# Moving the second copy of the un-normed result's high half from ScalarE to GpSimd

## The chip, the cores and the metric

The kernel runs on one core of one Trainium2 chip. The metric is the device time of that core in microseconds (us); the time given is the median of three runs. One more execution was profiled, and all rows below come from it. Batches, pairs, steps, blocks and rope operations are counted from 0; the steps' pairs are numbered through all batches, 0 to 31.

## The reference, cut to what matters

One transformer layer on x of shape (4, 1024, 256): a layer norm, multi-head latent attention with 16 heads, and beside it a linear layer with binarised weights. Both are added to x.

```
xn = layernorm(x)
kv_c = xn @ W_kvd + b_kvd                    # 64 wide
q_c  = xn @ W_qd + b_qd                      # 192 wide
keys_c, values = heads(kv_c @ W_ku + b_ku), heads(kv_c @ W_vu + b_vu)   # 16 heads x 128
keys_r = rope(heads(kv_c @ W_kr + b_kr))     # 16 heads x 64
queries_c, queries_r = heads(q_c @ W_qu + b_qu), rope(heads(q_c @ W_qr + b_qr))
scores = (concat(queries) @ concat(keys).T) / sqrt(192), causal
ctx = softmax(scores) @ values
x + ctx @ W_o + b_o + (xn @ binarised(W_ffn).T + b_ffn)
```

All is computed in float32 precision: a number is split into a high half (fp32r) and a low half (the number less its high half), and products are added up as high x high, high x low and low x high.

## The kernel before, in words

Weights are folded in a prologue (to about 130 us), so that attention works in the 64-wide space of kv_c. Then comes the main part: 4 batches x 8 pairs of heads = 32 steps m; each step has 4 blocks n, so there are 128 blocks g = 4m + n. A block takes two tiles of 128 queries, w = 0 (the long one) and w = 1 (the short one), for both heads of the pair. Every engine has its own `sequence(g)`, an order of calls written out by hand for n = 0, 1, 2 and 3. The calls name earlier blocks too: in block g TensorE works on the scores of g, turns and weighs the probabilities of g - 1 and g - 2, and makes the output of g - 2 and g - 3.

What one (block, w) passes through at its end:

- TensorE's `weigh_group` (L1369, L1370) adds up probabilities times kv_c in the PSUM tile `u_ps`: the un-normed result u, two heads side by side.
- ScalarE's `u_high` (L707) writes its high half to `u_hi[w]`, 128 partitions x 256.
- DVE's `u_low` (L941) writes the low half of the upper 64 partitions to partitions 0 to 63 of `u_pair[w]`.
- ScalarE's `u_again` (L716) copies partitions 0 to 63 of `u_hi[w]` to partitions 64 to 127 of `u_pair[w]`, the second copy of the high half. It counts up `u_copied`.
- TensorE's `output` waits for `u_ready` (from DVE) and `u_copied`, multiplies with the folded values' weights (L1389, L1390) into `o_ps`, and DVE's `accumulate` (L971) adds that to the result.

GpSimd (POOL) works in the main part on the rotary positions of the next pair: `step(m)` prepares pair m + 1. Its chain is ten `rope` operations, numbered 0 to 9 (L301), and two `low_keys` (L311), in the order rope 0, 1, 2, low_keys 1, rope 3, 4, 5, 6, 7, 8, low_keys 0, rope 9. rope 0 waits for the first swap of halves (`swapped<-k_rope`, four DMAs from SyncE's queue), rope 3 for the second (`swapped<-q_x`, `q_y`), which SyncE starts when ScalarE has evacuated the query projection q_y (L621). low_keys 1 waits for `k_hi` (L671) and rope 8 and 9 for `q_hi` (L675), all from ScalarE; ScalarE's `high_queries` in turn wait for rope 6 and 7. The next pair's scores on TensorE wait for rope 8, low_keys 0 and rope 9. In pair 5 of each batch but the last, `residual` (L456, eight additions) follows behind rope 9; in pairs 3 and 4 a few small operations and in pair 6 `down_low` stand in the chain too.

Every semaphore wait on an engine holds back all that is written behind it there.

Of the kernel before, what the change touches and what calls it, by code (L numbers as in the profile page):

```python
# [26 lines left out]
F32 = mybir.dt.float32  # L27
F32R = mybir.dt.float32r
BF16 = mybir.dt.bfloat16
ACT = mybir.ActivationFunctionType  # L30
# [4 lines left out]
P = 128  # L35
NB, SEQ, HID = 4, 1024, 256
# [32 lines left out]
STEPS = NB * PAIRS  # L69
# [25 lines left out]
def is_block(g):  # L95
    return 0 <= g < STEPS * BLOCKS
# [22 lines left out]
def build(nc, x, W_kvd, b_kvd, W_ku, b_ku, W_vu, b_vu, W_kr, b_kr, W_qd, b_qd, W_qu, b_qu, W_qr, b_qr,  # L119
# [6 lines left out]
    with ExitStack() as ctx:  # L126
# [320 lines left out]
        def _(pool):  # L447
# [43 lines left out]
            def down_low(b, k):  # L491
# [3 lines left out]
                pool.wait_ge(down_lo, b * 2 + k + 1)  # L495

            def step(m):

                b, pair = divmod(m, PAIRS)
                more = b + 1 < NB  # L500
                if m + 1 == STEPS:
                    return
                rope(pool, m + 1, range(0, 3))
                low_keys(pool, m + 1, 1)
                if more and pair in (3, 4):
                    pool.wait_ge(k_lo_ready, (m + 1) * 2 + 1)
                    (combine, refine)[pair - 3](b + 1)
                rope(pool, m + 1, range(3, 8))
                if more and pair == 6:
                    pool.wait_ge(rope_step, (m + 1) * ROPE_OPS + 8)  # L510
                    down_low(b + 1, 0)
                    down_low(b + 1, 1)
                rope(pool, m + 1, range(8, 9))
                low_keys(pool, m + 1, 0)
                rope(pool, m + 1, range(9, 10))
                if more and pair == 5:
                    pool.wait_ge(rope_step, (m + 1) * ROPE_OPS + ROPE_OPS)
                    residual(b + 1)
                    pool.wait_ge(residual_ready, (b + 2) * NT)
# [77 lines left out]
        def _(act):  # L597
# [106 lines left out]
            def u_high(g, w):  # L704
                if is_block(g):
                    act.wait_ge(u_full, g * 2 + w + 1)
                    act.activation(u_hi[w][:, :], u_ps[:, 0:2 * P], ACT.Identity).then_inc(u_hi_ready, 1)  # L707
                if w == 1 and (g + 1) % (PAIRS * BLOCKS) == 0 and g + 1 < STEPS * BLOCKS:
                    natural_high((g + 1) // (PAIRS * BLOCKS))

            def u_again(g, w):

                if not is_block(g):
                    return
                act.wait_ge(u_hi_ready, g * 2 + w + 1)
                act.activation(u_pair[w][64:P, :], u_hi[w][0:64, :].bitcast(F32), ACT.Identity).then_inc(u_copied, 1)  # L716

            def sequence(g):

                b, pair, n = g // (PAIRS * BLOCKS), g // BLOCKS % PAIRS, g % BLOCKS  # L720
                if n == 0:
                    evacuate(g, ROPE_K)
                    turned_high(g - 1, 0)
                    u_again(g - 2, 0)
                    u_high(g - 2, 1)
# [9 lines left out]
                    u_high(g - 1, 0)  # L735
                    u_again(g - 2, 1)
                    exponent(g, 2)
                    turned_high(g - 1, 4)
                    u_again(g - 1, 0)
                    if pair == 6:  # L740
# [11 lines left out]
                elif n == 1:  # L752
                    exponent(g, 0)
                    u_again(g - 2, 1)
                    if pair == 6:
# [8 lines left out]
                    if pair == 5:  # L764
                        next_apply(b + 1, 3)
                    u_again(g - 1, 0)
                    if pair == 4:
# [5 lines left out]
                elif n == 2:  # L773
                    exponent(g, 0)
                    turned_high(g - 1, 3)
                    if pair == 6:
                        next_down_high(b + 1, 1)
                    u_again(g - 2, 1)
                    exponent(g, 1)
# [8 lines left out]
                    turned_high(g, 0)  # L788
                    u_again(g - 1, 0)
                    high_queries(g, 0)  # L790
                    u_high(g - 1, 1)
                    turned_high(g, 1)
                else:
# [7 lines left out]
                    if pair == 5:  # L801
                        next_left("transpose", b + 1, 1)
                    u_again(g - 2, 1)
                    turned_high(g - 1, 4)
# [807 lines left out]
```

## Time and profile before

| what | value |
|---|---|
| median of 3 runs | 1487.29 us (1485.34 to 1489.63) |
| the profiled execution | 1487.06 us, of which its span is 1485.3 us |
| TensorE matmul busy | 1416.0 us, 95% |
| DVE busy | 1155.7 us, 78% |
| ScalarE (ACT) busy | 1204.2 us, 81% |
| GpSimd (POOL) busy | 981.4 us, 66% |

The span is what the rows cover, from the first instruction to the last; 1.8 us of the time lie outside it. In a row of a timeline the first number is the start and the second the duration, in us; in square brackets stands how long the engine was idle before it, and who released it. PE is the matmul and PEld the weight load of TensorE.

### The profile page before, as it was taken

To read this page: it belongs to the slowest core of one execution; us is meant where nothing else is said; L and a number is where in the kernel's file an instruction comes from. 1 tells how busy PE (TensorE), PEld (TensorE's weight loads), DVE (VectorE), ACT (ScalarE), POOL (GpSimd) and SP (SyncE) were. 2 spreads that over 40 slices of the span, in tenths; PEclk is the share of its full clock that TensorE was granted. 3 is DMA by queue.
4 is the path that set the end of the run, shared out by engine and by line. 5 is a ranking of instruction groups with operands and counts; after the bars stand their busy time and mean duration, and the time that the engine had idled before them with its cause. 6 is when DMAs were issued, how large, how long until landed. Compare 5 with 4: busy or idle time off the path is not lost.

```text
span 1485.3 us, 27605 instructions
## 1 busy us (share of the span) xinstructions
PE 1416.0 (95%) x9849; PEld 1281.7 (86%) x9849; DVE 1155.7 (78%) x2755; ACT 1204.2 (81%) x2553; POOL 981.4 (66%) x553
## 2 busy tenths in 40 slices
PE   3688999999999999999999999999999999999997
PEld 3467899999799989999889998999889999989987
DVE  2465888888677889888677888888677888878888
ACT  2345888899788888899778898889868888888886
POOL 5254777777656777777766777776767677677750
PEclk9778999999999999999999999999999999999999
DMA  8545121222142232211233221222132422211110
GB/s 232 172 138 153 49 76 43 60 61 61 54 111 64 69 89 62 61 54 55 61 72 100 78 86 51 61 61 61 46 74 67 111 61 62 62 46 42 49 30 29
DMA packets 41550, 110.48 MB, mean 74 GB/s; under 512 B 7574, under 2 KB 18119, under 8 KB 41415
## 3 DMA queue, kind: packets, MB, share of 16 engines
q1 hardware_dynamic: 37126, 95.09, 24.1%
q0 software_dynamic: 3232, 12.58, 2.4%
q8 instruction: 80, 1.31, 0.4%
q10 hardware_dynamic: 1056, 1.05, 0.3%
q14 instruction: 56, 0.45, 0.1%
HBM read 48.92 MB, written 13.63 MB: 42 GB/s over the span
## 4 chain that ended last, share of the span: by engine, by line
PE 76%; ACT 8%; POOL 5%; DVE 4%; DMA 3%; issue 2%; SPq 1%; POOLq 0%; DVEq 0%; ACTq 0%
PE turn L1351 14%; PE ring L1296 10%; PE u_ps L1369 7%; PE ring L1328 7%; PE ring L1326 7%; PE ring L1327 7%; PE u_ps L1370 7%; PE o_ps L1389 3%; PE o_ps L1390 3%; ACT probs L693 3%; PE ring L1258 2%; PE ring L1250 2%; PE ring L1309 2%; ACT probs_hi L702 1%; POOL k_rope L301 1%
## 5 line engine op out<-in xcount | busy, mean ns | idle before, releaser
L925 DVE TENSOR_SCALAR_CACHE_REDUCE probs<-ring,c_t 128x1024 f32<-128x1024 f32 (+7 forms) x512 | 413.8, 809 | 105.1 <-PE ring L1328 100.9
L935 DVE TENSOR_TENSOR probs_lo<-turn,probs_hi 128x512 fp32r<-128x512 f32 (+1 forms) x640 | 401.5, 631 | 70.0 <-ACT probs_hi L702 64.8
L702 ACT ACTIVATE probs_hi<-turn 128x512 fp32r<-128x512 f32 (+1 forms) x640 | 350.5, 550 | 113.2 <-PE turn L1351 107.4
L693 ACT ACTIVATE probs<-probs,row_min 128x1024 f32<-128x1024 f32 (+7 forms) x512 | 394.3, 771 | 12.1 <-DVE probs L925 9.6
L1351 PE MATMUL turn<-ident,probs 128*128 128x128 f32 x2304 | 386.2, 275 | 9.6 <-ACT probs L693 7.3
L1351 PEld LDWEIGHTS turn<-ident,probs 128*128 128x128 f32 x2304 | 285.9, 140 | 37.5 <-ACT probs L693 13.4
L1369 PE MATMUL u_ps<-probs_hi,kv_nat 128*128 128x256 f32 x1152 | 314.6, 302 | 0.3 <-DVE probs_lo L935 0.3
L1370 PE MATMUL u_ps<-probs_lo,kv_nat 128*128 128x256 f32 x1152 | 289.3, 281 | 0.0
L1326 PE MATMUL ring<-k_hi,q_hi 128*128 128x512 f32 (+2 forms) x768 | 280.2, 365 | 0.0
L1328 PE MATMUL ring<-k_hi,q_lo 128*128 128x512 f32 (+2 forms) x768 | 264.0, 344 | 0.0
L1327 PE MATMUL ring<-k_lo,q_hi 128*128 128x512 f32 (+2 forms) x768 | 263.4, 343 | 0.0
L971 DVE SCALAR_TENSOR_TENSOR acc<-o_ps,row_inv,acc 128x256 f32<-128x256 f32 x480 | 230.4, 480 | 34.6 <-PE o_ps L1390 30.2
L1369 PEld LDWEIGHTS u_ps<-probs_hi,kv_nat 128*128 128x128 f32 x1152 | 219.3, 190 | 1.7 <-DVE probs_lo L935 0.5
L1370 PEld LDWEIGHTS u_ps<-probs_lo,kv_nat 128*128 128x128 f32 x1152 | 218.6, 190 | 0.0
L311 POOL TENSOR_TENSOR k_lo<-k_rope,k_hi 64x1024 fp32r<-64x1024 f32 x62 | 148.2, 2391 | 51.5 <-ACT k_hi L671 49.1
L301 POOL TENSOR_TENSOR k_rope<-k_rope,cos 128x1024 f32<-128x1024 f32 x31 | 74.4, 2401 | 156.5 <-DMA swapped<-k_rope 156.3
L301 POOL TENSOR_TENSOR q_x<-q_x,cos 64x1024 f32<-64x1024 f32 x31 | 74.2, 2395 | 136.1 <-DMA swapped<-q_x 136.1
L1328 PEld LDWEIGHTS ring<-k_hi,q_lo 128*128 128x128 f32 x768 | 145.1, 189 | 13.9
L1326 PEld LDWEIGHTS ring<-k_hi,q_hi 128*128 128x128 f32 x768 | 146.9, 191 | 7.4
L301 POOL TENSOR_TENSOR swapped<-swapped,sin 128x1024 f32<-128x1024 f32 x62 | 148.8, 2401 | 4.9
L1327 PEld LDWEIGHTS ring<-k_lo,q_hi 128*128 128x128 f32 x768 | 145.8, 190 | 7.2
L1389 PE MATMUL o_ps<-wv,u_hi 128*128 128x256 f32 x512 | 143.4, 302 | 4.3 <-DVE acc L971 2.3
(210 smaller groups left out, 2607.8 us busy)
## 6 DMA issues: line engine op xcount, KB each, us to landing
wp<-wp_scratch SPq DMA_DIRECT2D x31, 640.0 KB, 4.2
swapped<-k_rope SPq DMA_DIRECT2D x128, 128.0 KB, 2.3
wv<-wv_scratch SPq DMA_DIRECT2D x31, 512.0 KB, 3.4
swapped<-q_y SPq DMA_DIRECT2D x64, 128.0 KB, 2.3
swapped<-q_x SPq DMA_DIRECT2D x64, 128.0 KB, 2.4
wp_scratch<-wp_parts POOLq DMA_DIRECT2D x7, 640.0 KB, 3.5
x_sb<-in_L_attn_x SPq DMA_DIRECT2D x4, 1024.0 KB, 6.5
k_hi<-qb_kv_hi SPq DMA_DIRECT2D x16, 256.0 KB, 3.7
```

What stands on the lines that cost most here:

```text
L301: engine.tensor_tensor(to, a, b, op).then_inc(rope_step, 1)
L693: act.activation(p, p, ACT.Exp, scale=-1.0, bias=row_min[:, r:r + 1], accum_out=row_sum[:, g % 4, w, h:h + 1]).then_inc(exp_ready, 1)
L702: act.activation(probs_hi[:, r % 4, 0:width], turn[r % 2][:, 0:width], ACT.Identity).then_inc(turned_hi, 1)
L925: dve.tensor_scalar(probs_of(g, w, h), ring[slot_of(entry)][:, KEY_COLUMN[qt]:KEY_COLUMN[qt] + keys], c_t[b % 2][:, qt, ds(pair * 2 + h, 1 ...
L935: dve.tensor_tensor(probs_lo[:, r % 4, 0:width], turn[r % 2][:, 0:width], probs_hi[:, r % 4, 0:width].bitcast(F32), ALU.subtract).then_inc ...
L971: dve.scalar_tensor_tensor(out=acc[:, qt, :], in0=o_ps[:, h, :], scalar=inv, in1=start[:, qt, :], op0=ALU.mult, op1=ALU.add).then_inc((acc ...
L1326: pe.matmul(to, qh, kh[:, keys], start=not masked, stop=False, skip_group_check=masked)
L1327: pe.matmul(to, qh, kl[:, keys], start=False, stop=False, skip_group_check=masked)
L1328: mm = pe.matmul(to, ql, kh[:, keys], start=False, stop=True, skip_group_check=masked)
L1351: mm = pe.transpose(turn[r % 2][:, (2 * t + h) * P:(2 * t + h + 1) * P], probs_of(g, w, h)[:, kt * P:(kt + 1) * P], ident[:, :])
L1369: pe.matmul(u_ps[:, 0:2 * P], kv_nat[:, kt, :], probs_hi[:, r % 4, cols], start=(kt == 0), stop=False)
L1370: mm = pe.matmul(u_ps[:, 0:2 * P], kv_nat[:, kt, :], probs_lo[:, r % 4, cols], start=False, stop=(kt == qt))
```

## The change: what it does

`u_again` leaves ScalarE's sequence in all its places and becomes a function of GpSimd's program, a `tensor_copy`. GpSimd makes eight such copies in a step: (g - 2, 0) and (g - 2, 1) before rope 0, (g - 1, 0) behind rope 0, (g - 1, 1) behind low_keys 1, (g, 0) behind rope 3, (g, 1) behind rope 4, (g + 1, 0) behind rope 6 and (g + 1, 1) behind rope 7, where g is the first block of the step. A copy waits for the rope operation before it, for `u_hi_ready`, for the output of the block before (`o_full`), and then for its own end (`u_copied`). ScalarE's `u_high` gets a wait for the copy of the block before, since its tile is now read on another engine.

```diff
@@ -494,18 +494,47 @@
                                    ALU.subtract).then_inc(down_lo, 1)
                 pool.wait_ge(down_lo, b * 2 + k + 1)
 
+            def u_again(g, w, roped=None):
+
+                if not is_block(g):
+                    return
+                if roped is not None:
+                    pool.wait_ge(rope_step, roped)
+                pool.wait_ge(u_hi_ready, g * 2 + w + 1)
+                if g >= 1:
+
+                    pool.wait_ge(o_full, g * 2 + w - 1)
+                pool.tensor_copy(u_pair[w][64:P, :], u_hi[w][0:64, :].bitcast(F32)).then_inc(u_copied, 1)
+                pool.wait_ge(u_copied, g * 2 + w + 1)
+
             def step(m):
 
                 b, pair = divmod(m, PAIRS)
-                more = b + 1 < NB
+                more, g, roped = b + 1 < NB, m * BLOCKS, (m + 1) * ROPE_OPS
+                u_again(g - 2, 0, m * ROPE_OPS + ROPE_OPS)
+                u_again(g - 2, 1)
                 if m + 1 == STEPS:
+                    for later in range(g - 1, STEPS * BLOCKS):
+                        for w in range(2):
+                            u_again(later, w)
                     return
-                rope(pool, m + 1, range(0, 3))
+                rope(pool, m + 1, range(0, 1))
+                u_again(g - 1, 0, roped + 1)
+                rope(pool, m + 1, range(1, 3))
                 low_keys(pool, m + 1, 1)
+                pool.wait_ge(k_lo_ready, (m + 1) * 2 + 1)
+                u_again(g - 1, 1)
                 if more and pair in (3, 4):
                     pool.wait_ge(k_lo_ready, (m + 1) * 2 + 1)
                     (combine, refine)[pair - 3](b + 1)
-                rope(pool, m + 1, range(3, 8))
+                rope(pool, m + 1, range(3, 4))
+                u_again(g, 0, roped + 4)
+                rope(pool, m + 1, range(4, 5))
+                u_again(g, 1, roped + 5)
+                rope(pool, m + 1, range(5, 7))
+                u_again(g + 1, 0, roped + 7)
+                rope(pool, m + 1, range(7, 8))
+                u_again(g + 1, 1, roped + 8)
                 if more and pair == 6:
                     pool.wait_ge(rope_step, (m + 1) * ROPE_OPS + 8)
                     down_low(b + 1, 0)
@@ -704,16 +733,12 @@
             def u_high(g, w):
                 if is_block(g):
                     act.wait_ge(u_full, g * 2 + w + 1)
+                    if g >= 1:
+
+                        act.wait_ge(u_copied, g * 2 + w - 1)
                     act.activation(u_hi[w][:, :], u_ps[:, 0:2 * P], ACT.Identity).then_inc(u_hi_ready, 1)
                 if w == 1 and (g + 1) % (PAIRS * BLOCKS) == 0 and g + 1 < STEPS * BLOCKS:
                     natural_high((g + 1) // (PAIRS * BLOCKS))
-
-            def u_again(g, w):
-
-                if not is_block(g):
-                    return
-                act.wait_ge(u_hi_ready, g * 2 + w + 1)
-                act.activation(u_pair[w][64:P, :], u_hi[w][0:64, :].bitcast(F32), ACT.Identity).then_inc(u_copied, 1)
 
             def sequence(g):
 
@@ -721,7 +746,6 @@
                 if n == 0:
                     evacuate(g, ROPE_K)
                     turned_high(g - 1, 0)
-                    u_again(g - 2, 0)
                     u_high(g - 2, 1)
                     turned_high(g - 1, 1)
                     if pair == 4:
...
```

The seven other calls of `u_again` in ScalarE's `sequence` are removed likewise.

The first place is GpSimd's program from rope 5 of pair 6 of the first batch (`swapped,sin`), past the residual, to the first operations for pair 7. Before:

```order
L301 TENSOR_TENSOR swapped<-swapped,sin 128x1024
L301 TENSOR_TENSOR q_x<-q_x,swapped 64x1024
L301 TENSOR_TENSOR q_y<-q_y,swapped 64x1024
L301 TENSOR_TENSOR q_lo<-q_x,q_hi 128x1024
L311 TENSOR_TENSOR k_lo<-k_rope,k_hi 64x1024
L301 TENSOR_TENSOR q_lo<-q_y,q_hi 128x1024
L456 TENSOR_TENSOR x_sb<-x_sb,bias_out 128x256 x8
L301 TENSOR_TENSOR k_rope<-k_rope,cos 128x1024
L301 TENSOR_TENSOR swapped<-swapped,sin 128x1024
```

The same place now, where L507 is the copy:

```order
L301 TENSOR_TENSOR swapped<-swapped,sin 128x1024
L301 TENSOR_TENSOR q_x<-q_x,swapped 64x1024
L507 CAST u_pair<-u_hi 64x256
L301 TENSOR_TENSOR q_y<-q_y,swapped 64x1024
L507 CAST u_pair<-u_hi 64x256
L301 TENSOR_TENSOR q_lo<-q_x,q_hi 128x1024
L311 TENSOR_TENSOR k_lo<-k_rope,k_hi 64x1024
L301 TENSOR_TENSOR q_lo<-q_y,q_hi 128x1024
L456 TENSOR_TENSOR x_sb<-x_sb,bias_out 128x256 x8
L507 CAST u_pair<-u_hi 64x256 x2
L301 TENSOR_TENSOR k_rope<-k_rope,cos 128x1024
L507 CAST u_pair<-u_hi 64x256
```

Two copies stand inside the chain here (two more stand ahead of the piece, behind `q_x,cos` and `q_y,cos`), and the two that end the step's blocks stand behind the residual.

The second place is ScalarE's program around the start of that same pair (the row `k_rope<-ring,bias_p` is the first call of a step). Before:

```order
L716 ACTIVATE u_pair<-u_hi 64x256
L702 ACTIVATE probs_hi<-turn 128x256
L693 ACTIVATE probs,row_sum<-probs,row_min 128x640
L707 ACTIVATE u_hi<-u_ps 128x256
L693 ACTIVATE probs,row_sum<-probs,row_min 128x512
L621 ACTIVATE k_rope<-ring,bias_p 128x1024
L702 ACTIVATE probs_hi<-turn 128x512
L716 ACTIVATE u_pair<-u_hi 64x256
L707 ACTIVATE u_hi<-u_ps 128x256
```

Now:

```order
L731 ACTIVATE probs_hi<-turn 128x256
L722 ACTIVATE probs,row_sum<-probs,row_min 128x640
L739 ACTIVATE u_hi<-u_ps 128x256
L722 ACTIVATE probs,row_sum<-probs,row_min 128x512
L650 ACTIVATE k_rope<-ring,bias_p 128x1024
L731 ACTIVATE probs_hi<-turn 128x512
L739 ACTIVATE u_hi<-u_ps 128x256
```

The copies are gone from ScalarE and nothing else changes its place there. The order on TensorE, DVE and SyncE is the same as before.

## Rows read from the trace of the kernel before

**Rows 1.** Stretch 170 to 1430: busy us (instructions) by engine, TensorE clock, DMA, GB/s.

```profile
170.00:1430.00 1260.00, 1247.62 (x8849) 1140.40 (x8848) 1021.69 (x2419) 1088.36 (x2286) 893.39 (x426) 1.00 0.25 66
```

**Rows 2.** Waits of the whole span: total us, times, longest us.

```profile
POOL q_x L301 <- DMA swapped<-q_x: 136.1, 31, 6.3
PE turn L1351 <- ACT probs L693: 7.3, 10, 1.1
```

**Rows 3.** Grouped lines of ScalarE: busy us, mean ns, idle before.

```profile
L716 ACT ACTIVATE u_pair<-u_hi 64x256 fp32r<-64x256 f32 x256 | 106.7, 417 | 6.2
```

**Rows 4.** Timeline, GpSimd, ScalarE, TensorE, around the start of pair 3.

```profile
217.20 1.12 ACT L621 ACTIVATE q_y<-ring,bias_p 128x1024 f32<-128x1024 f32 x1 [0.54 <-PE ring L1296]
222.64 2.39 POOL L301 TENSOR_TENSOR q_x<-q_x,cos 64x1024 f32<-64x1024 f32 x1 [4.51 <-DMA swapped<-q_x]
233.62 1.06 ACT L675 ACTIVATE q_hi<-q_x 128x1024 fp32r<-128x1024 f32 x1
240.01 2.39 POOL L301 TENSOR_TENSOR q_lo<-q_y,q_hi 128x1024 fp32r<-128x1024 f32 x1
240.43 0.37 ACT L707 ACTIVATE u_hi<-u_ps 128x256 fp32r<-128x256 f32 x1
243.02 0.42 ACT L716 ACTIVATE u_pair<-u_hi 64x256 fp32r<-64x256 f32 x1
244.23 0.37 PE L1389 MATMUL o_ps<-wv,u_hi 128*128 128x256 f32 x1
```

**Rows 5.** Grouped lines of GpSimd by form: busy us, mean ns.

```profile
L456 POOL TENSOR_TENSOR x_sb<-x_sb,bias_out 128x256 f32<-128x256 f32 x32 | 24.3, 799 | 0.2
L533 POOL CAST wp<-qr 128x128 fp32r<-128x128 f32 x2 | 0.6, 288 | 0.1
L534 POOL CAST wp<-kr 128x64 fp32r<-128x64 f32 x2 | 0.5, 230 | 0.0
```

**Rows 6.** Timeline, DVE and weight load, near the end.

```profile
1475.69 0.42 DVE L941 TENSOR_TENSOR u_pair<-u_ps,u_hi 64x256 fp32r<-64x256 f32 x1 [1.25 <-ACT u_hi L707]
1476.16 0.19 PEld L1389 LDWEIGHTS o_ps<-wv,u_hi 128*128 128x128 f32 x1 [1.13 <-DVE u_pair L941]
```

**Rows 7.** Timeline, last rope and output, at first and last of 17 boundaries.

```profile
200.63 2.39 POOL L301 TENSOR_TENSOR q_lo<-q_y,q_hi 128x1024 fp32r<-128x1024 f32 x1
204.43 0.36 PE L1389 MATMUL o_ps<-wv,u_hi 128*128 128x256 f32 x1
...
1392.30 2.40 POOL L301 TENSOR_TENSOR q_lo<-q_y,q_hi 128x1024 fp32r<-128x1024 f32 x1
1396.55 0.36 PE L1389 MATMUL o_ps<-wv,u_hi 128*128 128x256 f32 x1
```

**Rows 8.** Timeline, last rope and output at the start of pair 10.

```profile
544.68 2.41 POOL L301 TENSOR_TENSOR q_lo<-q_y,q_hi 128x1024 fp32r<-128x1024 f32 x1
547.59 0.37 PE L1389 MATMUL o_ps<-wv,u_hi 128*128 128x256 f32 x1
```

**Rows 9.** Timeline, GpSimd and TensorE around the first residual.

```profile
356.36 2.41 POOL L301 TENSOR_TENSOR q_lo<-q_x,q_hi 128x1024 fp32r<-128x1024 f32 x1 [0.81 <-ACT q_hi L675]
361.37 2.40 POOL L301 TENSOR_TENSOR q_lo<-q_y,q_hi 128x1024 fp32r<-128x1024 f32 x1
363.85 5.59 POOL L456 TENSOR_TENSOR x_sb<-x_sb,bias_out 128x256 f32<-128x256 f32 x8
366.71 0.36 PE L1389 MATMUL o_ps<-wv,u_hi 128*128 128x256 f32 x1
```

**Rows 10.** Timeline, last rope and output at the start of pair 8.

```profile
458.94 2.40 POOL L301 TENSOR_TENSOR q_lo<-q_y,q_hi 128x1024 fp32r<-128x1024 f32 x1
466.36 0.36 PE L1389 MATMUL o_ps<-wv,u_hi 128*128 128x256 f32 x1
```

**Rows 11.** Stretches around 1144, columns as in Rows 1.

```profile
1142.00:1144.00 2.00, 1.06 (x12) 0.83 (x9) 1.61 (x4) 0.97 (x3) 1.92 (x2) 1.00 0.03 8
1145.40:1148.80 3.40, 3.40 (x17) 3.40 (x17) 1.89 (x5) 2.10 (x5) 2.98 (x2) 0.51 0.00 0
```

More of the change, by code:

```diff
@@ L735, in sequence @@
                     u_high(g - 1, 0)
-                    u_again(g - 2, 1)
                     exponent(g, 2)
                     turned_high(g - 1, 4)
-                    u_again(g - 1, 0)
                     if pair == 6:
@@ L753, in sequence @@
                     exponent(g, 0)
-                    u_again(g - 2, 1)
                     if pair == 6:
@@ L765, in sequence @@
                         next_apply(b + 1, 3)
-                    u_again(g - 1, 0)
                     if pair == 4:
@@ L777, in sequence @@
                         next_down_high(b + 1, 1)
-                    u_again(g - 2, 1)
                     exponent(g, 1)
@@ L788, in sequence @@
                     turned_high(g, 0)
-                    u_again(g - 1, 0)
                     high_queries(g, 0)
@@ L802, in sequence @@
                         next_left("transpose", b + 1, 1)
-                    u_again(g - 2, 1)
                     turned_high(g - 1, 4)
```

## Prediction

> **What bounds the kernel now.** I read the busy time by stretch first. In the main part TensorE's matmuls are busy for 1247.6 of 1260 us at the full granted clock of 2.4 GHz, ScalarE for 1088.4 and GpSimd for 893.4 [rows 1]. TensorE sets the time; all its waits there come to 12.4 us. ScalarE has slack on average, and so has GpSimd. Taking work from ScalarE can give back no more than a share of those 12.4 us, while whatever makes TensorE wait comes on top in full. So the question is when the copies are finished now, and when TensorE asks for them.
>
> The list of waits comes next. GpSimd waits 136.1 us in 31 times for the second swap, 4.4 us each, and TensorE's longest item behind ScalarE is 7.3 us [rows 2]. GpSimd's idle time thus lies before rope 3. The timeline of an ordinary pair shows what follows [rows 4]: from rope 3 at 222.64 to rope 9 at 240.01 eight operations run with no gap, 17.37 us or seven times 2.48, so the chain is GpSimd's own from there on. It ends at 242.40, and TensorE starts the output of block g - 2, w = 0 at 244.23. ScalarE had finished u_hi for it at 240.80 and made the copy at 243.02 to 243.44, in time.
>
> **ScalarE's part.** It loses 256 operations of 417 ns, 106.7 us [rows 3]. None of that lies on the path by itself. What it can return are TensorE's waits, at most 12.4 us [rows 1]. Those behind ScalarE's probabilities are 7.3 us in all, the prologue's included [rows 2], and I take 4 us back.
>
> **The price of a copy on GpSimd.** No row shows this copy. The nearest are GpSimd's casts to fp32r: 288 ns for 128 elements, 230 ns for 64 [rows 5], a slope of 0.9 ns an element, which extends to 0.41 us for 256. The lower end is 0.29 us, the cast with half as many elements; the upper is the 256-element addition with its 0.80 us mean [rows 5]. A larger price because partitions 0 to 63 go to 64 to 127 isn't excluded either, and is held to be inside the upper end. I take 0.41, from the nearest rows in kind. With 0.07 us for the next instruction's start (2.48 less the 2.39 to 2.41 of an operation) a copy inside the chain moves all behind it by 0.48 us.
> The Trainium skill's page GPSIMD Engine Reference, section 4.1, Engine selection, speaks against elementwise work on GpSimd, about twice as slow with two inputs, but holds one input to be roughly line rate. [...] No run here shows it yet.
>
> **Where the copies fall.** Five matter. Four stand between rope 3 and rope 9, and move the end of rope 9 by 4 x 0.48 = 1.92 us. The one that TensorE asks for next, (g - 2, 0) of the next step, stands behind rope 9, though its u_hi has long been there. It ends 0.07 + 0.41 later; a weight load starts 0.05 us after what it waits for [rows 6], and I allow 0.04 more to its matmul. So the output can start 2.49 us after the end of rope 9 in the old timeline. The old timeline gives it less:
>
> - Ordinary boundaries between two pairs: 1.83 us at pair 3 [rows 4], 1.41 at the first of them and 1.85 at the last [rows 7]. There are 17 (pairs 2 to 5, 9, 11 to 13, 17, 18, 20, 21, 25 to 27, 29 and 30). TensorE comes to wait 0.66, 1.08 and 0.64 us at those three. Where rope 8 had waited for q_hi (5, 13, 21) the chain takes up part of the slip. I take 0.6 us as the mean: 17 x 0.6 = 10.2.
> - Five boundaries with less room (1, 10, 19, 28, 31), as the second swap came late: 547.59 - 547.09 = 0.50 us at pair 10 [rows 8]. TensorE waits 2.0 there: 5 x 2.0 = 10.0.
> - Three boundaries with the residual between rope 9 and the copy (6, 14, 22). Rope 9 ends at 363.77, the residual takes 5.59 + 0.08 on top, and the output stood at 366.71, which is 2.94 us behind rope 9 [rows 9]. The copy allows it at 5.67 + 2.49 = 8.16, less 0.74 of the 0.81 us that rope 8 had waited [rows 9]: a wait of 8.16 - 0.74 - 2.94 = 4.48. 3 x 4.5 = 13.5.
> - Six with room to spare (7, 8, 15, 16, 23, 24): 5.02 us at pair 8 [rows 10]. Nothing.
>
> The sum is 33.7 us. The chain of the next pair starts from a swap that follows TensorE's projections and ScalarE's evacuation, so each wait shifts TensorE and the next chain together; the next boundary is short by the same amount again, not by more or less.
>
> **The clock.** In the stretch 1142 to 1144 TensorE is busy 1.06 of 2 us, and 1145.4 to 1148.8 runs at a granted 0.51, its 1.2 GHz level [rows 11]. Half speed over 3.4 us costs 1.7 us. The three waits of 4.5 us are longer than that idle stretch, so I add 3 x 1.7 = 5.
>
> **What I count at nothing.** Rope 2 ends one copy (0.48 us) later, and k_hi with it; ScalarE's 0.54 us wait for the projection of q_y covers this [rows 4]. With no cover it would be 0.5 us in 31 pairs, 15 us. The second swap on SyncE's queue waits for rope 2 too, but the evacuation of q_y ends at 218.32 [rows 4], long behind it. Rope 6 ends at 222.64 + 4 x 2.48 - 0.08 = 232.48 and now 0.96 later, at 233.44, before ScalarE came to q_hi at 233.62 [rows 4]. The wait added to `u_high` is for a copy of a block earlier, done by then; behind it on ScalarE stand the probabilities' high halves, for which DVE and TensorE wait. The last step has no rope, and a copy there ends about when DVE's half does.
>
> **The sum.** 1487.1 (profiled execution) + 33.7 + 5 - 4 = 1521.8, and as the median of the runs stands 0.2 us above that execution, 1522 us. The ends of the copy's price: 0.12 us less in five places at some 22 boundaries is 13 less; 0.39 more at 25 boundaries is about 45 more (five copies x 0.39 = 1.95 each, less a little where there is room).
>
> **Rivals.**
> - Dear copies: the price near the upper end, 1487 + 34 + 45 + 5 - 4 = 1567. For it: GpSimd's 799 ns mean at this width [rows 5]. Against it: that is two inputs, and the casts lie on a line far below.
> - The clock falls at ordinary boundaries as well: 22 more falls of 1.7 us, 37 us, 1559. For it: a stretch with 0.94 of 2 us idle came before the fall [rows 11]. Against: the main part holds several such waits, and its mean clock is 1.00 [rows 1]. The Trainium skill's page TensorE: Matmul & The Clock Gate, part 1, says that the clock follows how busy TensorE has been of late and drops to half after idleness; the trace agrees with 0.51 granted behind the stretch that was 0.94 us idle.
> - Faster: ScalarE, 3.3 us lighter in a pair, evacuates earlier, the second swap lands earlier and the chain starts earlier by more than the copies add; then TensorE's waits shrink as well, down to 1487 - 12 = 1475. The place is rope 3, and it decides from 0.7 us of lead at the ordinary boundaries. Against it: ScalarE waits for TensorE before q_y [rows 4], so it has no lead to give, and the residual's 4.5 us would stay in any case.
> - No change: the same lead, but only large enough for the ordinary boundaries to balance the residual's. Nothing in the rows gives it.
>
> **How the numbers follow.** My forecast 0.68, dear copies 0.13, clock at ordinary boundaries 0.08, faster 0.06, no change 0.05. A measurement of this kernel tells 0.3%, 4.5 us, from no change. Faster by more than that 0.06, within it 0.05, slower 0.89. The range runs from the cheap copy with no fall of the clock and a little more given back, 1487 + 34 - 13 - 4 - 4 = 1500, to the neighbourhood of both dear cases, 1562.
>
> **What would show it.** In the profile after: a copy on GpSimd of about 0.41 us; TensorE idle before L1389's successor, released by GpSimd's copy, about 25 times, 34 us in all, three of them 4 to 5 us long at the starts of pairs 6, 14 and 22 with the granted clock below 1 behind them; ScalarE busy 107 us less and idle more. I am wrong if GpSimd's copies release TensorE almost never (the chain started earlier), if a copy takes 0.3 or 0.8 us, or if TensorE's new waits are for ScalarE's k_hi or q_hi.

## The result and the profile after

The changed kernel takes 1544.65 us (median of 4 runs, 1543.47 to 1552.24) against 1486.32 (1482.51 to 1489.63) beside it: a ratio of 1.0408, 95% interval 1.037 to 1.0445. It is slower by 58.3 us, where 35 were forecast. The profiled execution is the slowest of the four, 1552.24 us with a span of 1550.4, 65.2 us above the profiled one of before.

The busy times of the page after (engine, busy us, share of the span, instructions):

```profile
PE 1439.8 (93%) x9849; PEld 1297.2 (84%) x9849; DVE 1154.3 (74%) x2755; ACT 1097.0 (71%) x2297; POOL 1081.6 (70%) x809
```

ScalarE is busy 107.2 us less and GpSimd 100.2 us more. The main part, columns as in [rows 1], is 60 us longer for nearly the same work:

```profile
170.00:1490.00 1320.00, 1267.98 (x8846) 1152.39 (x8846) 1018.73 (x2417) 988.26 (x2047) 984.63 (x663) 0.99 0.24 63
```

TensorE is idle 52.0 us there, where it was 12.4 in [rows 1], and busy 20.4 us more. Its work is the same; 17.1 of the 20.4 us are a slower clock, as shown below, and 3.3 are left without a cause. The copy, as the page groups it, answers to [rows 3]; the columns are those of rows 3 with the releaser at the end:

```profile
L507 POOL CAST u_pair<-u_hi 64x256 fp32r<-64x256 f32 x256 | 100.9, 394 | 139.6 <-ACT u_hi L739 91.8
```

A copy takes 0.394 us. GpSimd idled 91.8 us for `u_hi` at its head, a wait that did not exist; 37.2 us of it lie in the last 60 us, where no rope operation stands behind the copies. The list of waits, columns as in [rows 2]:

```profile
POOL q_x L301 <- DMA swapped<-q_x: 97.3, 30, 5.7
POOL u_pair L507 <- ACT u_hi L739: 91.8, 23, 6.9
PE o_ps L1406 <- issue: 24.6, 14, 5.2
PE ring L1313 <- issue: 23.2, 4, 11.1
ACT q_hi L704 <- POOL q_x L301: 24.9, 25, 2.3
ACT k_hi L700 <- POOL k_rope L301: 20.8, 28, 1.9
ACT k_rope L650 <- POOL k_lo L311: 13.4, 21, 0.7
```

GpSimd's wait for the second swap is 39 us shorter than in [rows 2], and a new one of 91.8 us for `u_hi` stands beside it. ScalarE waits longer for GpSimd: 24.9 us for the rope operation ahead of `q_hi` (6.3 before) and 20.8 ahead of `k_hi` (10.7 before), and its wait for low_keys 0 ahead of `k_rope` is new. TensorE waits at the output (L1406, before L1389) and at a projection of the next pair (L1313, before L1296); one of the four waits at L1313, of 11.1 us, lies in the prologue. "issue" says that the profile names no releaser there; the timelines do.

**An ordinary boundary.** The timeline from pair 26 to 27, to be laid beside [rows 4, 7]:

```profile
1312.61 2.40 POOL L301 TENSOR_TENSOR q_x<-q_x,cos 64x1024 f32<-64x1024 f32 x1 [3.17 <-DMA swapped<-q_x]
...
1329.27 2.39 POOL L311 TENSOR_TENSOR k_lo<-k_rope,k_hi 64x1024 fp32r<-64x1024 f32 x1
1331.80 2.40 POOL L301 TENSOR_TENSOR q_lo<-q_y,q_hi 128x1024 fp32r<-128x1024 f32 x1
1334.26 0.85 POOL L507 CAST u_pair<-u_hi 64x256 fp32r<-64x256 f32 x2
...
1331.76 1.12 ACT L650 ACTIVATE k_rope<-ring,bias_p 128x1024 f32<-128x1024 f32 x1 [0.61 <-POOL k_lo L311]
1332.77 0.59 ACT L731 ACTIVATE probs_hi<-turn 128x512 fp32r<-128x512 f32 x1
...
1333.39 0.69 DVE L952 TENSOR_TENSOR probs_lo<-turn,probs_hi 128x512 fp32r<-128x512 f32 x1 [1.38 <-ACT probs_hi L731]
...
1334.14 0.33 PE L1368 MATMUL turn<-ident,probs 128*128 128x128 f32 x1 [0.21 <-DVE probs_lo L952]
1334.76 0.36 PE L1406 MATMUL o_ps<-wv,u_hi 128*128 128x256 f32 x1
```

The chain from the start of rope 3 to the end of rope 9 is 1334.20 - 1312.61 = 21.59 us against 242.40 - 222.64 = 19.76: 1.83 us more for four copies. It delays TensorE in two ways. ScalarE's evacuation of `k_rope` (L650) may overwrite only when low_keys 0 (L311) has read, so it waits 0.61 us; the high halves of the probabilities, their low halves and TensorE's transposes follow it late, 0.36 us when the instructions of both traces are laid side by side. Then the copy behind rope 9 delays the output, another 0.36. The copy has the last word: at all 22 boundaries that are neither a residual's nor within two pairs behind it, the output starts 0.56 us behind the end of rope 9, where it was 0.48 to 2.08 us before. Most boundaries of this kind are 0.4 to 0.7 us longer than before; those of pairs 2, 9, 17 and 25 are 1.1 to 1.5 us longer, those of 4 and 13, which have a late second swap, 2.7 and 3.4, and those of 5 and 21, where rope 8 had waited for `q_hi`, 0.1 and 0.2.

**Where the residual stands.** The same place as [rows 9]:

```profile
371.41 2.39 POOL L301 TENSOR_TENSOR q_lo<-q_y,q_hi 128x1024 fp32r<-128x1024 f32 x1
373.88 5.50 POOL L456 TENSOR_TENSOR x_sb<-x_sb,bias_out 128x256 f32<-128x256 f32 x8
379.45 0.85 POOL L507 CAST u_pair<-u_hi 64x256 fp32r<-64x256 f32 x2
...
379.94 0.55 PE L1406 MATMUL o_ps<-wv,u_hi 128*128 128x256 f32 x1 [5.19 <-issue]
```

The output starts 0.10 us after the first copy's end (379.45 + 0.39). It waits 5.19 us here, 5.20 and 5.16 in the two later batches. The matmul then takes 0.55 us for 0.36: the clock fell.

**Where the next batch starts.** The timeline of pair 6, GpSimd, SyncE's queue and TensorE:

```profile
415.25 2.37 POOL L301 TENSOR_TENSOR q_x<-q_x,swapped 64x1024 f32<-64x1024 f32 x1
422.00 0.39 POOL L507 CAST u_pair<-u_hi 64x256 fp32r<-64x256 f32 x1 [4.38 <-ACT u_hi L739]
422.47 2.39 POOL L301 TENSOR_TENSOR q_y<-q_y,swapped 64x1024 f32<-64x1024 f32 x1
424.93 0.39 POOL L507 CAST u_pair<-u_hi 64x256 fp32r<-64x256 f32 x1
425.40 2.35 POOL L493 TENSOR_TENSOR qa_lo<-xn,qa_hi 128x1024 fp32r<-128x1024 f32 x1
427.83 2.38 POOL L493 TENSOR_TENSOR qb_kv_lo<-xn,qb_kv_hi 128x1024 fp32r<-128x1024 f32 x1
...
430.25 0.50 SPq L358 DMA_DIRECT2D kv_stack<-qb_kv_hi  x1
...
437.05 1.81 PE L1313 MATMUL ring<-kv_stack,wp 128*128 128x512 f32 x4 [4.00 <-issue]
```

And the same three steps before, where nothing stood between rope 6 and `down_low` (L493) but rope 7:

```profile
395.80 2.35 POOL L301 TENSOR_TENSOR q_x<-q_x,swapped 64x1024 f32<-64x1024 f32 x1
398.23 2.34 POOL L301 TENSOR_TENSOR q_y<-q_y,swapped 64x1024 f32<-64x1024 f32 x1
400.65 2.41 POOL L493 TENSOR_TENSOR qa_lo<-xn,qa_hi 128x1024 fp32r<-128x1024 f32 x1
403.70 2.37 POOL L493 TENSOR_TENSOR qb_kv_lo<-xn,qb_kv_hi 128x1024 fp32r<-128x1024 f32 x1 [0.64 <-ACT qb_kv_hi L651]
...
417.39 1.09 PE L1296 MATMUL ring<-kv_stack,wp 128*128 128x512 f32 x4
```

From rope 6 to `down_low` it was 4.85 us and is now 10.15. The copy of (g + 1, 0) waits 4.38 us for its `u_hi`, and everything behind it on GpSimd waits too. `down_low` makes the low half of the next batch's compressed input; SyncE starts the transfer that builds `kv_stack` (430.25) only when it is done (427.83 + 2.38), and TensorE's first projection of the next batch reads `kv_stack`. It comes after 4.00 us of waiting (4.04 and 4.10 in the later batches), and its four matmuls take 1.81 us for 1.09.

The clock in two stretches, one behind the first wait of each kind:

```profile
381.00:388.00 7.00, 7.00 (x31) 5.97 (x31) 2.48 (x7) 2.49 (x6) 1.88 (x2) 0.63 0.00 1
437.00:441.00 4.00, 3.95 (x18) 3.63 (x18) 0.97 (x2) 1.51 (x2) 1.01 (x2) 0.57 0.02 4
```

Added up over the main part, TensorE spent 37.5 us at 1.2 GHz where it was 3.4 before: 6.8, 3.4 and 6.8 us behind the three waits at the output, 3.4, 6.8 and 6.8 behind the three at the projection, and 3.4 at pair 24, where the kernel before had them too [rows 11]. At half speed the 34.1 us more are 17.1 us lost.

### The profile page after: what moved, and what is told of

It reads as the page before. It is cut to its first block and busy times, and to the rows that moved or that the text cites. A ratio compares the mean times of both kernels' runs of the same rounds, so it can differ in the third digit from the quotient of the medians.

```text
span 1550.4 us, 28267 instructions
## 1 busy us (share of the span) xinstructions
PE 1439.8 (93%) x9849; PEld 1297.2 (84%) x9849; DVE 1154.3 (74%) x2755; ACT 1097.0 (71%) x2297; POOL 1081.6 (70%) x809
## 5 line engine op out<-in xcount | busy, mean ns | idle before, releaser
L1368 PEld LDWEIGHTS turn<-ident,probs 128*128 128x128 f32 x2304 | 289.8, 142 | 36.1 <-DVE probs_lo L952 15.5
L507 POOL CAST u_pair<-u_hi 64x256 fp32r<-64x256 f32 x256 | 100.9, 394 | 139.6 <-ACT u_hi L739 91.8
L311 POOL TENSOR_TENSOR k_lo<-k_rope,k_hi 64x1024 fp32r<-64x1024 f32 x62 | 147.8, 2383 | 50.1 <-ACT k_hi L700 42.7
L1406 PE MATMUL o_ps<-wv,u_hi 128*128 128x256 f32 x512 | 145.6, 306 | 31.5 <-issue 24.6
```

Source lines behind the costliest of these rows:

```text
L1368: mm = pe.transpose(turn[r % 2][:, (2 * t + h) * P:(2 * t + h + 1) * P], probs_of(g, w, h)[:, kt * P:(kt + 1) * P], ident[:, :])
```

## The experiments

To see where a run gains or loses, I took the times of the output (g - 2, 0) at the starts of pairs 1 to 29 in each profile, and summed how much longer the period up to it is than before, in us (the period up to pair 1 counts from the first output of all). Pairs 6, 14, 22 are where the residual stands; the periods that end with pairs 7, 15, 23 hold `down_low` and the first projection of the next batch; 23 others remain.

| profile of | pairs 6, 14, 22 | 7, 15, 23 | 23 others | sum |
|---|---|---|---|---|
| the changed kernel | +15.7 | +24.1 | +18.6 | +58.4 |
| e1, down_low first | +15.4 | +8.5 | +13.2 | +37.1 |
| e2, copy before residual | -1.2 | +17.2 | +13.6 | +29.6 |
| e3, both | -0.5 | +3.0 | +13.1 | +15.6 |
| e4, only (g + 2, 0) on ScalarE | -0.5 | +17.4 | +8.8 | +25.8 |
| e5, before without the copies | -1.6 | -1.7 | -9.8 | -13.1 |
| e6, before with a longer chain | +1.8 | -0.1 | +11.8 | +13.5 |
| e7, three copies | 0.0 | -0.1 | -2.4 | -2.5 |
| e8, six copies | -1.0 | -1.7 | -0.1 | -2.8 |
| e9, eight copies, low_keys 0 early | -1.3 | +3.0 | -2.0 | -0.3 |
| e10, low_keys 0 early alone | +0.5 | 0.0 | +3.0 | +3.6 |
| e11, seven copies, low_keys 0 early | -2.0 | -1.7 | -2.1 | -5.8 |
| e12, five copies, low_keys 0 early | 0.0 | 0.0 | +2.4 | +2.4 |

Each row is one profiled execution; that of the changed kernel is 7.6 us above its median. Two things move single periods without being an effect of the copies there. The 3.4 us at half speed that the kernel before has in the period of pair 24 lie elsewhere or nowhere in some runs (-1.6 us at pair 24, +1.5 to +1.6 at pair 8 or 16 where they lie there). And a late second swap, which the kernel before has for pairs 10, 19 and 28, falls on other pairs.

My theory after the result: three costs of place. The copy behind the residual, the two copies ahead of `down_low`, and the ordinary boundary. The rivals: a general loss (contention, or ScalarE's new waits) that would stay whatever is moved, and a clock that falls of itself.

**e1: in pair 6 `down_low` goes ahead of the copies (g + 1, 0) and (g + 1, 1).**

```diff
-                u_again(g + 1, 0, roped + 7)
+                if not (more and pair == 6):
+                    u_again(g + 1, 0, roped + 7)
                 rope(pool, m + 1, range(7, 8))
-                u_again(g + 1, 1, roped + 8)
                 if more and pair == 6:
...
                     down_low(b + 1, 1)
+                    u_again(g + 1, 0)
+                u_again(g + 1, 1, roped + 8)
```

> As the kernel after, but in pair 6 of a batch GpSimd makes down_low right behind rope 7, and the copies (g + 1, 0) and (g + 1, 1) behind it. Theory A (places: TensorE waits only where it asks for a copy, or for what stands behind one): in the kernel after, down_low stands behind copies that wait for u_hi, TensorE's first projection of the next batch starts 4.0 us late three times, and the clock falls to its 1.2 GHz level behind that for 3.4 us or more. That goes: 3 x (4.0 + 1.7) = 17 us, 1544.7 - 17 = 1528 (1524 to 1532). Theory B (the rotary chain as a whole is too long now, 1.8 us in every pair, and TensorE waits for rope and low_keys): down_low's place does not matter, 1541 to 1548.

Measured: 1528.51 us (1528.24 to 1529.76), ratio 1.0291 (1.0269 to 1.0313), 16.1 us below the changed kernel. In the timeline of pair 6 `down_low` follows rope 7 without a gap and the projection has no wait:

```profile
417.05 2.39 POOL L301 TENSOR_TENSOR q_y<-q_y,swapped 64x1024 f32<-64x1024 f32 x1
419.52 2.39 POOL L493 TENSOR_TENSOR qa_lo<-xn,qa_hi 128x1024 fp32r<-128x1024 f32 x1
...
433.81 1.09 PE L1315 MATMUL ring<-kv_stack,wp 128*128 128x512 f32 x4
```

**e2: in pair 5 the copy (g + 2, 0) goes ahead of the residual** (and is left out at the next step's start).

```diff
                 if more and pair == 5:
+                    u_again(g + 2, 0, roped + ROPE_OPS)
                     pool.wait_ge(rope_step, (m + 1) * ROPE_OPS + ROPE_OPS)
                     residual(b + 1)
```

> As the kernel after, but in pair 5 of a batch GpSimd makes the copy (g + 2, 0) behind rope 9 and ahead of the residual. Theory A: TensorE's three waits of 5.2 us at the start of pair 6 shrink to the ordinary 0.6 us, and the fall of the clock behind them (6.8 us at half speed, 3.4 us) goes: 3 x (4.1 + 3.4) = 22 us, 1522 (1517 to 1527). Theory B: within 4 us of 1544.7.

Measured: 1519.41 us (1517.33 to 1523.16), ratio 1.023 (1.0207 to 1.0253), 25.2 us below the changed kernel. The long waits at pairs 6, 14 and 22 are gone (+15.7 became -1.2), and 7 us of the 24.1 at pairs 7, 15 and 23 went with them: those periods begin at half speed.

**e3: both.**

> Both moves together. Theory A: the two places are apart in time and add up, 17 + 22 = 39 us: 1506 (1500 to 1512), which leaves about 17 ordinary boundaries of 0.65 us and some late swaps, 20 us over the kernel before. Theory B: 1538 to 1546.

Measured: 1510.65 us (1508.94 to 1511.63), ratio 1.0167 (1.0148 to 1.0186). Two moved lines return 34.0 of 58 us. Time at half speed is back to 3.4 us, now in the period of pair 16. At pair 6 the copy stands ahead of the residual and the output does not wait:

```profile
370.42 2.40 POOL L301 TENSOR_TENSOR q_lo<-q_y,q_hi 128x1024 fp32r<-128x1024 f32 x1
372.88 0.39 POOL L507 CAST u_pair<-u_hi 64x256 fp32r<-64x256 f32 x1
373.35 5.57 POOL L456 TENSOR_TENSOR x_sb<-x_sb,bias_out 128x256 f32<-128x256 f32 x8
...
373.54 0.36 PE L1410 MATMUL o_ps<-wv,u_hi 128*128 128x256 f32 x1
```

Alone the two edits give 16.1 and 25.2, together 34.0, 7.3 less than the sum. The table shows the same 7.3 (21.3 and 28.8 alone, 42.8 together): 4.9 of it is at the 23 others, where each edit alone takes away about 5 us and both together no more (the late swap at pair 13, +3.4 us, is gone in all three), and only 1.4 at pairs 7, 15 and 23, where half speed behind the first wait and the second wait overlap. What is left, 13.1 of 15.6 us, lies at the other boundaries. A general loss is out as the cause of the 34 us; whether the rest is one, e6 and e8 tell.

**e4: the copy (g + 2, 0) of every step back on ScalarE, in its old place; the rest as in the changed kernel.** It takes away the copy behind rope 9 and behind the residual at once. ScalarE has a count of its own for its copies.

```diff
+def on_pool(g, w):
+
+    return (g % BLOCKS, w) != (2, 0)
...
-                pe.wait_ge(u_copied, count + 1)
+                pe.wait_ge(u_copied if on_pool(g, w) else u_copied_act, copies_until(g, w))
```

> As the kernel after, but of the eight copies of a step the one that TensorE asks for first in the next pair, (g + 2, 0), is made by ScalarE in its old place; down_low stays behind its copies. Theory A: the waits at the ordinary boundaries (17 x 0.65 = 11 us) and at the residual's with their clock (3 x 8.1 = 24) go, those before the next batch (17 us) and some of late swaps stay: 1544.7 - 35 = 1510 (1504 to 1516). Theory B: one copy less behind the chain and none less inside it, 1540 to 1546.

Measured: 1520.75 us (1515.59 to 1523.63), ratio 1.0232 (1.0205 to 1.026). A miss by 11 us. The residual's places are clean (-0.5), but the others keep 8.8 us. At an ordinary boundary the 0.36 us at the output is gone, but the delay at the transposes has stayed (0.4 us when laid side by side), with this item in the list of waits:

```profile
ACT k_rope L662 <- POOL k_lo L323: 13.1, 21, 0.7
```

That led to a second theory: the longer chain itself costs, through low_keys 0 and the evacuation of `k_rope`, wherever the copy that TensorE asks for stands.

**e5 and e6 take the change apart.** e5 is the kernel before with the second copy left out in all blocks but the first, so ScalarE is relieved and GpSimd does nothing new. TensorE's wait for the copy is left out with it.

```diff
                 if not is_block(g):
                     return
+                if g > 0:
+                    return
                 act.wait_ge(u_hi_ready, g * 2 + w + 1)
```

> The kernel before with the second copy left out on every engine but in block 0, so that the upper half of u_pair is stale from then on. It shows what ScalarE's relief is worth by itself. My theory: TensorE sets the time, at most part of its 12.4 us of waits comes back: 1482 (1476 to 1486). A rival, that ScalarE's queue holds TensorE back inside its busy time too, would give 1465 or less, and the change would then have hidden a large gain.

Measured: 1472.66 us (1471.65 to 1473.88), ratio 0.9907 (0.9894 to 0.9919), 14 us less than before, where I had expected 4. But 5.0 us of it come from only three periods (-1.5, -1.8, -1.7 us, at pairs 10, 19 and 28), those with a late second swap in the kernel before, and e10 below gains 1.3 and 1.5 us at pairs 10 and 19 with every copy still on ScalarE. So those 5 us are not shown to be the relief, and about 9 are left for it. Nor are the 12.4 us of [rows 1] a ceiling: from the first output to that of pair 29 TensorE is idle 5.7 us less than before and also busy 7.3 us less, with the same 8480 matmuls and the same 3.4 us at half speed. Part of what ScalarE costs it stands inside its busy time, as the rival had it, though far less than the rival's 20 us.

e6 is the kernel before with a dummy addition (0.39 us were meant, 0.373 measured) on GpSimd at each place of a copy, waiting for nothing but the chain; ScalarE keeps its copies.

```diff
+                pool.tensor_tensor(idle_sum[:, :], bias_out[:, 0:88], bias_out[:, 88:176], ALU.add).then_inc(idle_done, 1)
+                pool.wait_ge(idle_done, g * 2 + w + 1)
```

> The kernel before, with ScalarE's copies where they were, and at the places of the kernel after a small addition of 0.39 us on GpSimd into a tile that nobody reads (88 elements of the output's bias). The rotary chain is 1.8 us longer as in the kernel after, but TensorE waits for no copy of GpSimd and the additions wait for no u_hi. Theory A as first put (TensorE waits only for copies): 1486 to 1489. Theory A2, from the traces of after and of the run with one copy back on ScalarE (0.36 us of each ordinary boundary is ScalarE's evacuation of k_rope, which waits for low_keys 0 of the chain and holds back the probabilities' high halves): 17 x 0.36 = 6 us, and up to 2 us at each of the five boundaries behind a late second swap: 1496 (1492 to 1502). Theory B (the chain's length is all): 1520 or more.

Measured: 1505.63 us (1501.68 to 1511.35), ratio 1.0139 (1.0118 to 1.016), above the range that I had given the second theory (the profiled execution, with +13.5 us in the table, is the fastest of its six, 1501.68). The length of the chain alone costs 19 us: 0.3 to 0.7 at most ordinary boundaries, 1.6 to 2.0 at pairs 1, 4, 22 and 28. The wait is the one that e4 had shown, here in the timeline of the 27th boundary:

```profile
1284.17 1.11 ACT L647 ACTIVATE k_rope<-ring,bias_p 128x1024 f32<-128x1024 f32 x1 [0.38 <-POOL k_lo L312]
```

**e7 and e8 choose which copies GpSimd makes.** e7 gives it the three that lie outside the chain (rope 3 to rope 9): (g - 2, 1), (g - 1, 0) behind rope 2, and (g - 1, 1). e8 gives it all but (g + 1, 0) and (g + 2, 0), with (g - 1, 0) behind rope 2 and `down_low` first.

```diff
+    return g % BLOCKS == 3 or (g % BLOCKS, w) == (2, 1)      # e7
+    return (g % BLOCKS, w) not in ((2, 0), (1, 0))           # e8
```

> GpSimd makes three of the eight copies of a step: (g - 2, 1) ahead of rope 0, (g - 1, 0) behind rope 2 and (g - 1, 1) behind low_keys 1. All three lie where GpSimd waited in the kernel before, outside the stretch from rope 3 to rope 9. The other five stay on ScalarE. All theories that put the loss into the chain or into copies behind it: no loss, 1484 (1479 to 1488). If a GpSimd copy costs TensorE something wherever it stands, 1492 or more.

> GpSimd makes six of the eight: all but (g + 1, 0) and (g + 2, 0), which are ScalarE's again; (g - 1, 0) stands behind rope 2 and down_low ahead of (g + 1, 1). Three copies (1.4 us) are left in the chain ahead of low_keys 0. Theory A2: ScalarE came to the evacuation of k_rope 1.5 us behind low_keys 0 in the kernel before (239.87 and 241.40), so three copies just fit and TensorE asks for none that is late: 1487 (1483 to 1493), the little that is lost being at late swaps. Theory A as first put: the same. Theory B: three quarters of a chain's slip of 1.8 us in each pair, 1520 or more.

Measured: e7 1484.29 us (1481.6 to 1488.81), ratio 0.9992 (0.998 to 1.0003); e8 1487.68 us (1481.25 to 1490.4), ratio 1.0004 (0.999 to 1.0018). Both as expected, and both the kernel before within what can be measured. Six copies of eight on GpSimd cost nothing that shows, so no general loss is left.

**e9 to e12 take the chain's own cost away.** low_keys 0 is moved from behind rope 8 to right behind low_keys 1, so that `k_rope` is free before rope 3. e9 has this with all eight copies, with (g - 1, 0) behind rope 2, `down_low` first and the copy ahead of the residual; e10 is the kernel before with this move alone; e11 is e9 with (g + 1, 0) on ScalarE; e12 leaves ScalarE (g, 0), (g, 1) and (g + 1, 0).

```diff
                 low_keys(pool, m + 1, 1)
+                low_keys(pool, m + 1, 0)
...
                 rope(pool, m + 1, range(8, 9))
-                low_keys(pool, m + 1, 0)
                 rope(pool, m + 1, range(9, 10))
```

> The full change with its three costs designed away: all eight copies on GpSimd, but low_keys 0 right behind low_keys 1 (where GpSimd waited 4.4 us for the second swap), which takes 2.5 us out of the chain between rope 3 and rope 9; (g - 1, 0) behind rope 2; down_low ahead of (g + 1, 0) and (g + 1, 1); (g + 2, 0) ahead of the residual. Theory A2 (the loss is three places: a chain 1.8 us longer that meets ScalarE's evacuation of k_rope and TensorE's output, the copy behind the residual, down_low behind copies): rope 9 ends 0.6 us before its old time instead of 1.9 behind it, the loss is gone and a good part of the 14 us of ScalarE's relief shows: 1479 (1474 to 1487). What may stay is (g + 1, 0), asked for 1.8 us behind the end of rope 6 in the kernel before and 1.4 us behind it at the least here. Theory C (copies on GpSimd cost something wherever they stand): 1500 or more.

> The kernel before with low_keys 0 right behind low_keys 1 and nothing else, the control for the run beside it. A2: the chain had slack there at the ordinary boundaries, so 1486 (1482 to 1488); the late second swaps may give 1 us each. If it gains 8 us or more, the gain of the full version is the keys' and not ScalarE's relief.

> As the version with all eight copies, but (g + 1, 0), the one that TensorE asks for soonest behind its rope operation, is ScalarE's again. A2: the last late copy goes; one eighth of the relief with it (2 us): 1478 (1473 to 1484). If it equals the version with eight within 2 us, that copy was in time.

> GpSimd makes (g + 1, 1), (g + 2, 0), (g + 2, 1), (g - 1, 0) and (g - 1, 1) of a step, ScalarE (g, 0), (g, 1) and (g + 1, 0), so rope 3 to rope 6 run without a copy between them and q_hi isn't later than before. A2: 1480 (1475 to 1485). It lies below the versions with seven or eight copies if ScalarE's wait for rope 6 (q_hi, 25 times in the kernel after) costs TensorE time, and above them if only the number of copies taken from ScalarE counts.

| run | median us | ratio, 95% interval |
|---|---|---|
| e9 | 1490.92 | 1.0025 (1.0014 to 1.0036) |
| e10 | 1491.67 | 1.0037 (1.0025 to 1.005) |
| e11 | 1484.51 | 0.9993 (0.9984 to 1.0002) |
| e12 | 1492.31 | 1.0038 (1.0026 to 1.0051) |

e9 returns 54 of the 58 us with every copy still on GpSimd: what the change cost was place. But all four lie above the ranges given, 12 us above the expected value in e9 and e12 and 6 in e11 and e10. e11, with (g + 1, 0) back on ScalarE, is 6.4 us faster than e9, mostly at pairs 7, 15 and 23 (+3.0 became -1.7), so that copy was late in e9. And e11 is 7.2 us faster than e10, which has the same early low_keys 0 and no copy on GpSimd: a relief of ScalarE shows, and the early low_keys 0 has used it up.

The move alone costs 5 us (e10), at pairs 8, 9, 16, 17 and 25 (+1.6, +1.3, +1.6, +1.7, +2.5 us). At pairs 8 and 16 it is the clock: 3.4 us at half speed each, where pair 24 has lost those of the kernel before (-1.6). At pairs 9, 17 and 25 TensorE has a wait that only e9 to e12 have (5.6 to 6.3 us in each, that of the first batch included):

```profile
PE u_ps L1369 <- DVE kv_nat L912: 6.1, 4, 1.7
```

It stands at the start of a batch, where DVE makes the low half of `kv_nat`. The timeline before, where GpSimd's low_keys 1 had ended at 824.57:

```profile
822.20 2.37 POOL L311 TENSOR_TENSOR k_lo<-k_rope,k_hi 64x1024 fp32r<-64x1024 f32 x1 [1.24 <-ACT k_hi L671]
825.10 0.69 DVE L912 TENSOR_TENSOR kv_nat<-xn_t,kv_nat 128x512 fp32r<-128x512 f32 x1
```

And in e10, where both low_keys run on GpSimd until 831.66:

```profile
826.82 4.84 POOL L311 TENSOR_TENSOR k_lo<-k_rope,k_hi 64x1024 fp32r<-64x1024 f32 x2 [1.24 <-ACT k_hi L671]
829.72 2.48 DVE L912 TENSOR_TENSOR kv_nat<-xn_t,kv_nat 128x512 fp32r<-128x512 f32 x1
832.26 0.38 PE L1369 MATMUL u_ps<-probs_hi,kv_nat 128*128 128x256 f32 x1 [1.66 <-DVE kv_nat L912]
```

In e9 to e12 the same DVE operation takes 2.08 to 2.74 us in all 16 batches, where it takes 0.69 in the ten other kernels, and it ends 0.55 us behind the end of low_keys 0 each time. So the two operations did not get on side by side here: low_keys 0, moved to a place where GpSimd was idle, now covers a DVE operation that TensorE waits for.

In e10 GpSimd's idle time ahead of rope 3 is no longer put down to the swap (136.1 us in [rows 2]), and is shorter, without a releaser that the profile names:

```profile
POOL q_x L301 <- issue: 55.1, 25, 3.8
```

e12 differs from e11 in (g, 0) and (g, 1) alone, which are ScalarE's again, and is 8 us slower. In the profiles 4.9 of 8.2 us lie at pairs 5, 6, 7, 14, 15, 21, 22 and 23. At pairs 5, 6, 7, 14 and 15 e12, e7 and e10, which leave these two copies on ScalarE, are within 0.2 us of the kernel before, while e5 and e11, which take them away, gain 0.5 to 0.8 us at each. So a good part of the relief hangs on these two copies; through which wait, I did not settle. No version that makes all the copies beats the kernel before by more than the measurement can tell.

## Why the prediction was right, and where it was off

- **What bounds the kernel**: right. TensorE sets the time, and what was lost in the main part is its idle time (39.6 us more) and its busy time (20.4 us more, 17.1 of them by the slower clock).
- **The price of a copy**: right. 0.394 us against 0.41, and four of them in the chain 1.83 us against 1.92. The rival of dear copies is out.
- **Ordinary boundaries**: right, but a second way is missing. The output starts 0.56 us behind rope 9, as 2.49 less 1.92 had it, and 0.6 us each was forecast where most lost 0.4 to 0.7. But the copy is not the only cause: without it (e4) 0.3 to 0.5 us stay at most of them, which come through low_keys 0 and the evacuation of `k_rope`, a wait that is absent from my list of what I counted at nothing. The evacuation had 1.5 us of room at pair 3 (low_keys 0 ended at 239.87, it began at 241.40), and the chain's slip of 1.5 us up to there uses it up. e4 and e6 showed it.
- **Boundaries with a late second swap**: the step stands on pairs that the changed kernel does not share. In the changed kernel pairs 4 and 13 have the late swap and lose 2.7 and 3.4 us; pairs 10, 19 and 28, which had it before, lose -0.4, 0.5 and 0.9. That the sum is near is luck: the 16 boundaries that I called ordinary up to pair 29 cost 16.3 us against 16 x 0.6 = 9.6, and the four late ones 2.4 against 8.0. With the others it is 18.6 us against 17.6.
- **Residual boundaries**: right. 15.7 us in three against 13.5, and e2 took them away.
- **The clock**: it fell behind the residual as forecast, but for longer: 6.8, 3.4 and 6.8 us at half speed, or 8.5 us lost against the term's 5 (13.7 us at half speed in e1, 6.8 lost). That it would fall at the next batch's start too was not in the term, which knew no wait there: 8.5 us more. The rival that it falls at ordinary boundaries too is out: in e3 the main part has 3.4 us at half speed, as before.
- **The start of the next batch**: the step that was missing, and the reason for 1544 in place of 1522. Pairs 7, 15 and 23 stood in my list as boundaries with nothing to lose, or six with room to spare; they cost 24.1 us, of which I had 5 in the clock's term. I had priced each copy by its duration and by what stands in front of it, and none by what stands behind it on GpSimd while it waits for `u_hi`: `down_low`, a transfer and TensorE's projection. The order of GpSimd's program that I read ended one step short of it. Up to pair 29 the forecast has 32.1 us (33.7 less 2.6 for pairs 30 and 31, and 5 less 4) and the profile 58.4: of the 26.3 us between them 19.1 are here, 2.2 at the residual, 1.0 at the others, and 4 are the relief that did not show.
- **The relief of ScalarE**: mis-sized. 4 us were forecast, at most 12.4, and e5 gives 14, of which about 9 are not at the late swaps. The ceiling was wrong in kind: half of the gain in e5 is busy time of TensorE. In the changed kernel it cannot be seen by itself, since ScalarE then waits for GpSimd (24.9, 20.8 and 13.4 us in the list of waits).
- **No change and faster**: out for this kernel. Without the two large waits it still loses 25 us (e3), and e9 comes near no change only with low_keys 0 moved as well.
- **The signs**: about 25 waits before the output with 34 us in all were forecast; the list has 14 with 24.6 us, three of them 5.2 us long. The profile names no releaser there instead of the copy.
- **The range**: that 1544 lies inside it is luck. Its upper part stood for dear copies and a clock that falls at ordinary boundaries, and both are out.

## What to carry to other kernels

Before moving a short operation to an engine with time to spare, list what stands behind it in that engine's order, and who waits for that; the operation's wait costs more than the operation (4.38 us against 0.39 here). Follow each releaser two steps on: a buffer that the lengthened chain frees late is a wait as well as a result that comes late. When an engine is relieved, price it by a run without the work, not by the waits that carry its name or by the idle time of the engine that sets the pace. And an engine's idle time is not free for every operation: in e10 low_keys 0, put into GpSimd's idle time, stretched a DVE operation that TensorE waits for.

## What the runs showed of the hardware

- GpSimd copies 64 x 256 elements from partitions 0 to 63 to 64 to 127 in 0.394 us, in line with its casts of the same kind on the same partitions (0.288 us for 128 elements, 0.230 for 64): that the partitions change costs nothing that can be seen.
- After the six waits of 4 to 5 us the granted clock was at its 1.2 GHz level for 6.8 us four times and for 3.4 us, as in [rows 11], twice. Over the main part that makes 17.1 us lost beside the 39.6 us of waits.
- A DVE subtraction with both inputs in SBUF (`kv_nat`, 0.69 us) took 2.08 to 2.74 us where GpSimd's low_keys 0 ran beside it (e9 to e12, 16 times of 16), and ended 0.55 us behind it; in the ten other kernels it took 0.69 to 0.70 us, 40 times of 40.
- The busy time of TensorE's matmuls is not free of what others do: in e5 8480 matmuls took 1189.7 us against 1197.0 at the same time of half speed.
- In the kernel before, three second swaps let rope 3 start 6.2 to 6.6 us behind the end of the evacuation, those that prepare pairs 10, 19 and 28 (and that of pair 1, 6.0), instead of the usual 4.3 to 4.4. In that stretch the list of queues has a packet of queue q8, of kind "instruction". In the fourteen profiles together 29 of 434 second swaps took more than 5.7 us by this measure, and all 29 have such a packet in the 4.3 us behind the evacuation. Of the 397 that took less than 5.0 us only three have one, each 3.8 us or more behind the evacuation's end; of the eight between, five. The two go together, then, and which pairs they fall on changes from kernel to kernel; that the packet is the cause, no run tested.
